# Query look-ups of an edge attention: one fp32 product a tile in place of three bf16 ones

## The chip, the core and the metric

One core of a Trainium2 chip runs one program. The core has TensorE (matrix products, written to PSUM), VectorE, ScalarE, GpSimd and SyncE, which run their own instruction streams and wait for each other by semaphores. The metric is the device time of one execution in microseconds; less is better.

## The reference

The program is a graph network of four parts over 3125 nodes with 128 features and 53125 edges (25000 random ones, their reverses, and a self-loop at each node), sorted by target `dst`: ten propagation steps, two graph attention layers, a relational layer, and a transformer layer on edges. Between the parts stands a layer norm of x plus the part's result. The change lies in the last two. The relational layer adds to x a weighted sum over edges and normalizes x. The attention then computes:

```
Q = (x @ Wq).reshape(n, 8, 16); K, V likewise
score = K[src] * Q[dst] / sqrt(16)
s = exp(clip(sum(score, -1), -5, 5))
wV = segment_sum(V[src] * s, dst); z = segment_sum(s, dst)
h = (wV / (z + 1e-6)) @ Wo + bo, then x + h, two batch norms and a two-layer MLP
```

## The kernel before

Nodes are cut into NB = 25 blocks of 128. The edges of a block fill CAP = 18 tiles of 128 edges, and 8 in the last block: 440 tiles. The blocks are also grouped into seven sets (five of 4 blocks, one of 2, one of 3); after a set the next part's matrix products for its nodes are slipped in between blocks.

**Relations** (L2246 to L2320). GpSimd gathers for each tile 128 rows from a table in HBM (L2265) into a ring `rows` of three blocks. VectorE makes one-hot matrices of the targets (L2299). TensorE adds up each tile by a product of the one-hot matrix with the rows (L2286), in fp32; after each six tiles (a group) a matmul increments `summed`, for which GpSimd waits before it reuses those slots of the ring. VectorE closes a block (L2307, L2309) and, at the end of a set, normalizes it. Then **IntoCross** makes keys, values and queries of that set: TensorE transposes x (L2185), ScalarE copies the transpose (L2205), TensorE multiplies each block by the three weight matrices together (L2193, 384 columns, two PSUM banks `pr` in turn), ScalarE copies the 384 columns into a ring `kvq` (L2215, semaphore `out`) and stores keys and values to a table in HBM (L2218). VectorE splits the queries into three bf16 parts whose sum is the fp32 value (L2232, L2235, L2238, L2241) into `own`, and increments `split`. In the last set keys and values come first and the queries after them (L2197, L2223).

**Cross** is the attention. Its engines run these loops over the blocks:

- GpSimd gathers keys and values of each tile (L2593) into the same ring `rows` of three blocks; each six tiles it waits for the sums that free the slots.
- SyncE sends the targets of a block, broadcast over the partitions, to `dst_wide`; ScalarE makes the transposed one-hot matrices `turned` of it by two passes (L1857, L1861), so that column e of `turned` picks the target's row for edge e.
- TensorE looks up the query of each edge: for each tile three bf16 matmuls with `turned` as the stationary operand and the three parts of the queries moving, added up in PSUM (L2623). Tiles are taken in groups of four (quads), five a block. The first three quads of block b + 1 are looked up before the sums of block b; the fourth and fifth come at the start of the next turn, since they reuse the banks of the first two. Each increments `looked`.
- VectorE multiplies the gathered keys by the looked-up queries (L2668), adds them up a head (L2673), clips (L2687), and, after ScalarE's exponentials (L2604, L2607), weighs the values (L2695), then makes the next one-hot matrices (L1824).
- TensorE adds up the weighed values (L2644, fp32, 136 columns). Every six tiles `summed` is incremented. VectorE closes the block (L2700 to L2702).

The order on TensorE in turn b is: quads 3 and 4 of block b, quads 0 to 2 of block b + 1, sums of block b. After each set of blocks some products of the next part come ahead of that.

```
            for j, tiles in enumerate(quads_of(b)):
                pe.wait_ge(self.ready, QUADS[b] + j + 1)
```

Of the kernel before, what the change touches and what calls it, by code (L numbers as in the profile page):

```python
# [1359 lines left out]
class Tiles:  # L1360


    def __init__(self, c, ctx, y):
# [45 lines left out]
        self.iota = self.top_ps[:, 384:384 + P]  # L1409
        self.weight = self.seen_ps[:, 432:432 + CAP * HEADS].rearrange("p (t h) -> p t h", h=HEADS)  # L1410

    def query(self, b):

        return self.own[:, b, :].bitcast(bf16)[:, 0:3 * D].rearrange("p (i f) -> p i f", i=3)
# [414 lines left out]
class TurnedHots:  # L1829
# [21 lines left out]
    def turn(self, act, b):  # L1851
# [9 lines left out]
        c.nc.scalar.activation(t.turned[:, b % 2, 0:n], t.apart[:, 0:n], ACT.Relu, bias=c.ones[:, 0:1], scale=-1.0).then_inc(self.turned_made, 1)  # L1861


class Layer(TurnedHots):
# [15 lines left out]
    def looked_after(self, b):  # L1880
        return b + 1

# [272 lines left out]
class IntoCross:  # L2155
# [3 lines left out]
    def __init__(self, c, t, table):  # L2159
        self.c, self.t, self.table = c, t, table  # L2160
        self.loaded, self.small, self.turned, self.copied, self.done, self.out, self.split, self.step = (
            c.sem(f"into_x_{n}") for n in ("loaded", "small", "turned", "copied", "products", "out", "split", "step"))
        self.tabled = [c.sem(f"into_x_tabled{h}") for h in range(2)]
        self.stored = [0, 0]
# [12 lines left out]
    def pe(self, pe, layer, i):  # L2177
# [11 lines left out]
        for j, b in enumerate(blocks):  # L2189
            if b >= 2:  # L2190
                pe.wait_ge(self.out, b - 1)
            n = 2 * D if at_end else 3 * D
            c.nc.tensor.matmul(t.pr[b % 2][:, 0:n], t.turned_all[:, j * P:(j + 1) * P], t.w_kvq[:, 0:n], start=True, stop=True).then_inc(self.done, 1)  # L2193
        if at_end:
            for j in range(len(blocks)):
                pe.wait_ge(self.out, NB + j - 1)
                c.nc.tensor.matmul(t.pr[(NB + j) % 2][:, 0:D], t.turned_all[:, j * P:(j + 1) * P], t.w_kvq[:, 2 * D:3 * D], start=True, stop=True).then_inc(self.done, 1)  # L2197

    def act(self, act, layer, i):
# [7 lines left out]
        n = 2 * D if at_end else 3 * D  # L2207
        for piece in pieces_of(blocks):
            half = piece[0] // 4 % 2
            for b in piece:  # L2210
                if b >= 8 and b % 4 == 0:
                    act.wait_ge(self.tabled[half], 16 * self.stored[half])
                    act.wait_ge(self.split, b // 4 - 1)
                act.wait_ge(self.done, b + 1)
                c.nc.scalar.copy(t.kvq[:, b % 8, 0:n], t.pr[b % 2][:, 0:n]).then_inc(self.out, 1)  # L2215
# [4 lines left out]
        if at_end:  # L2220
            for j, b in enumerate(blocks):
                act.wait_ge(self.done, NB + j + 1)
                c.nc.scalar.copy(t.kvq[:, b % 8, 2 * D:3 * D], t.pr[(NB + j) % 2][:, 0:D]).then_inc(self.out, 1)  # L2223

    def dve(self, dve, layer, i):
        c, t, blocks, v = self.c, self.t, SETS[i], self.c.nc.vector
        pieces = [(t.kvq[:, p[0] % 8:p[0] % 8 + len(p), 2 * D:], [t.own[:, p[0]:p[-1] + 1, :].bitcast(bf16)[:, :, n * D:(n + 1) * D] for n in range(3)])
                  for p in pieces_of(blocks)]
        dve.wait_ge(self.out, blocks[-1] + 1 + (len(blocks) if i == len(SETS) - 1 else 0))
        then = chained(dve, self.step, 3 * i)  # L2230
        for query, parts in pieces:
            last = v.tensor_copy(parts[0], query)  # L2232
        then(last)
        for query, parts in pieces:
            last = v.tensor_tensor(query, query, parts[0], ALU.subtract)  # L2235
        then(last)
        for query, parts in pieces:
            last = v.tensor_copy(parts[1], query)  # L2238
        then(last)
        for query, parts in pieces:  # L2240
            last = v.tensor_tensor(parts[2], query, parts[1], ALU.subtract)  # L2241
        last.then_inc(self.split, 1)


class Relations:
# [45 lines left out]
    def dve(self, dve, own_out):  # L2291
# [22 lines left out]
        for b in range(NB):  # L2314
            if b + 1 < NB:
                make_hots(b + 1)
            if b - 1 in SET_DONE:
                self.after.dve(dve, self, SET_DONE[b - 1])
            close(b)
        self.after.dve(dve, self, len(SETS) - 1)  # L2320
# [243 lines left out]
class Cross(TurnedHots):  # L2564
# [3 lines left out]
    def __init__(self, c, t, table, tabled, split, after):  # L2568
        self.c, self.t, self.table, self.tabled, self.split, self.after = c, t, table, tabled, split, after
# [6 lines left out]
    def looked_after(self, b):  # L2576
        return LOOKED[b + 1]

# [35 lines left out]
    def pe(self, pe):  # L2614
        c, t = self.c, self.t

        def look_up(b, lo, hi):
            pe.wait_ge(self.turned_made, b + 1)
            query = t.query(b)
            for j in range(lo, min(hi, len(quads_of(b)))):  # L2620
                for m, n in enumerate(quads_of(b)[j]):
                    for i in range(3):
# [985 lines left out]
```

## Time and profile before

| | |
|---|---|
| runs | 4167.31, 4172.69, 4187.54 us, median 4172.69 |
| profiled execution, span from first to last instruction | 4173.0 us (no other time is given for it) |
| TensorE, VectorE, GpSimd busy | 61%, 51%, 42% of the span |
| relation stage, first to last gather | 2781.0 to 3397.2 us |
| attention stage, first to last gather | 3423.3 to 4084.2 us |
| mean granted TensorE clock | 0.765 of full speed |

In the rows below PE is TensorE's matmuls and PEld its weight loads, DVE VectorE, ACT ScalarE, POOL GpSimd. The start of a matmul in the trace is when it entered TensorE's stream; its end is modelled. In brackets stands the idle time of the engine before an instruction and what ended it: "issue" means that it waited for nothing that the profile shows, "remote" that the releaser was not found.

### The profile page before, as it was taken

To read this page: it belongs to the slowest core of one execution; us is meant where nothing else is said; L and a number is where in the kernel's file an instruction comes from. 1 tells how busy PE (TensorE), PEld (TensorE's weight loads), DVE (VectorE), ACT (ScalarE), POOL (GpSimd) and SP (SyncE) were. 2 spreads that over 40 slices of the span, in tenths; PEclk is the share of its full clock that TensorE was granted. 3 is DMA by queue.
4 is the path that set the end of the run, shared out by engine and by line. 5 is a ranking of instruction groups with operands and counts; after the bars stand their busy time and mean duration, and the time that the engine had idled before them with its cause. 6 is when DMAs were issued, how large, how long until landed. Compare 5 with 4: busy or idle time off the path is not lost.

```text
span 4173.0 us, 49514 instructions
## 1 busy us (share of the span) xinstructions
PE 2540.6 (61%) x14597; PEld 1791.1 (43%) x14598; DVE 2114.5 (51%) x5736; ACT 725.1 (17%) x1115; POOL 1742.4 (42%) x1837
## 2 busy tenths in 40 slices
PE   5879999999996355565245555552333343444446
PEld 3546666666664244344134333432222232444445
DVE  8975555555554365566255455651222233444446
ACT  5840000000002132222122222210000011112112
POOL 2210000000002666664565555526666656666660
PEclk9989999999998677676567776775555665666667
DMA  2000000000004444442344343321111123333331
GB/s 63 1 1 0 0 0 0 0 0 0 0 0 123 112 118 125 116 123 78 109 116 125 113 117 112 112 60 47 50 52 52 52 70 104 105 109 107 109 112 28
DMA packets 139378, 283.86 MB, mean 68 GB/s; under 512 B 35752, under 2 KB 79124, under 8 KB 139156
## 3 DMA queue, kind: packets, MB, share of 16 engines
q0 software_dynamic: 77760, 204.68, 17.8%
q1 hardware_dynamic: 24603, 53.25, 4.0%
q10 hardware_dynamic: 36864, 24.07, 1.9%
q8 instruction: 76, 1.25, 0.1%
q14 instruction: 75, 0.61, 0.0%
HBM read 255.10 MB, written 27.01 MB: 68 GB/s over the span
## 4 chain that ended last, share of the span: by engine, by line
issue 20%; PE 14%; DVE 14%; another core or an unknown queue 11%; POOL 6%; ACT 2%; DMA 1%; SPq 0%; DVEq 0%; ACTq 0%; POOLq 0%
PE t_sum_ps L1996 7%; POOL t_rows L2265 6%; DVE t_onehot L1824 2%; PE t_product_ps L1665 2%; DVE t_rows L2078 2%; DVE t_stage L2668 1%; DVE t_stage L2673 1%; DVE t_rows L2695 1%; PE t_sum_ps L2286 1%; ACT t_apart L1857 1%; PE t_small_ps L1966 1%; PE t_product_ps L1590 0%; POOL t_rows L2593 0%; DVE t_norm_pair L1335 0%
## 5 line engine op out<-in xcount | busy, mean ns | idle before, releaser
L1896 POOL DMA_INDIRECT t_rows<-gat_table,t_src x880 | 837.9, 952 | 572.0 <-issue 254.0
L1038 PE MATMUL hop_ps<-parts,counts 128*128 128x384 bf16 (+1 forms) x6150 | 1003.3, 326 | 2.2 <-DVE parts L1099 2.2
L1038 PEld LDWEIGHTS hop_ps<-parts,counts 128*128 (+1 forms) x6150 | 603.4, 98 | 402.2 <-issue 10.2
L1996 PE MATMUL t_sum_ps<-t_rows,t_onehot 128*128 128x264 f32 x1760 | 540.6, 465 | 258.4 <-issue 210.3
L1996 PEld LDWEIGHTS t_sum_ps<-t_rows,t_onehot 128*128 128x128 f32 x1760 | 405.0, 234 | 367.9 <-issue 286.9
L2265 POOL DMA_INDIRECT t_rows<-rel_table_b,t_rel x440 | 418.9, 952 | 272.7 <-issue 129.8
L2593 POOL DMA_INDIRECT t_rows<-kv_table_b,t_src x440 | 416.0, 945 | 271.0 <-issue 127.0
L1465 POOL IOTA t_node<- 128x1 f32 x1 | 0.1, 131 | 1040.5 <-POOLq L106 1040.5
L2286 PE MATMUL t_sum_ps<-t_rows,t_onehot 128*128 128x128 f32 x880 | 174.6, 340 | 334.6 <-issue 283.9
L2286 PEld LDWEIGHTS t_sum_ps<-t_rows,t_onehot 128*128 128x128 f32 x880 | 155.7, 251 | 356.7 <-issue 356.2
L2644 PE MATMUL t_sum_ps<-t_rows,t_onehot 128*128 128x136 f32 x880 | 185.8, 366 | 152.9 <-issue 152.1
L2078 DVE TENSOR_TENSOR t_rows<-t_rows,t_sum_ps 128x768 f32<-128x768 f32 x288 | 253.2, 947 | 17.6 <-issue 9.8
L2668 DVE TENSOR_TENSOR t_stage<-t_rows,t_small_ps 128x512 f32<-128x512 f32 x98 | 58.6, 619 | 368.0 <-remote 332.5
L2644 PEld LDWEIGHTS t_sum_ps<-t_rows,t_onehot 128*128 128x128 f32 x880 | 169.2, 270 | 173.9 <-issue 173.4
L1107 DVE TENSOR_REDUCE s_new<-hop_ps 128x128 f32<-128x384 f32 (+1 forms) x225 | 125.5, 558 | 220.9 <-PE hop_ps L1038 212.2
L2623 PE MATMUL t_small_ps<-t_own,t_turned 128*128 128x128 bf16 x1032 | 90.3, 262 | 206.1 <-issue 180.3
L2307 DVE TENSOR_TENSOR t_own<-t_own,t_sum_ps 128x128 f32<-128x128 f32 x25 | 7.2, 287 | 407.8 <-remote 383.1
L1824 DVE TENSOR_TENSOR t_onehot<-t_small_ps,t_dst 128x768 f32<-128x768 f32 x222 | 196.9, 941 | 1.8 <-DVE y_fast L2099 0.6
L929 PE MATMUL cnt_ps<-hot_column,hot_src 128*128 128x320 bf16 x880 | 160.5, 320 | 39.1 <-DVE hot_column L973 34.9
L1474 ACT COPY t_turned_all<-t_turn_ps 128x512 f32<-128x512 f32 (+1 forms) x4 | 2.2, 558 | 1022.9 <-PE t_turn_ps L1508 1021.4
L2623 PEld LDWEIGHTS t_small_ps<-t_own,t_turned 128*128 128x128 bf16 x1032 | 81.5, 120 | 214.3 <-issue 192.2
L1857 ACT ACTIVATE t_apart<-t_dst_wide,t_node 128x2304 f16<-128x2304 f16 (+1 forms) x75 | 161.9, 2158 | 19.9 <-DMA t_dst_wide<-dst_row 19.6
(366 smaller groups left out, 3013.1 us busy)
## 6 DMA issues: line engine op xcount, KB each, us to landing
t_dst_wide<-dst_row SPq DMA_DIRECT2D x72, 576.0 KB
t_rows<-gat_table,t_src POOLq DMA_INDIRECT x880
rel_table_b<-t_stage ACTq DMA_DIRECT2D x25, 512.0 KB, 3.2
t_rows<-rel_table_b,t_rel POOLq DMA_INDIRECT x440
t_rows<-kv_table_b,t_src POOLq DMA_INDIRECT x440
gat_table<-t_own ACTq DMA_DIRECT2D x10, 520.0 KB, 6.5
kv_table_b<-t_fresh ACTq DMA_DIRECT2D x5, 512.0 KB
out<-x SPq DMA_DIRECT2D x6, 256.0 KB
```

What stands on the lines that cost most here:

```text
L929: last = nc.tensor.matmul(bank[:, h * 512:h * 512 + JH], hot_src[:, g % 2, :, n], hot[:, k % RING, h * JH:(h + 1) * JH], start=(k == ks[0] ...
L1038: last = nc.tensor.matmul(ps[bank][0:m, 0:PARTS * D], counts[:, k, columns], parts[old][:, k, :], start=(k == 0), stop=(k == NB - 1))
L1824: last = v.tensor_tensor(t.onehot[:, hot_at(ks[lo]):hot_at(ks[lo]) + m, :], t.iota.rearrange("p (o d) -> p o d", o=1).to_broadcast([P, m, P]),
L1857: c.nc.scalar.activation(t.apart[:, 0:n], t.dst_wide[:, b % 2, 0:n], ACT.Abs, bias=t.node[:, 0:1], scale=-1.0).then_inc(self.apart_made, 1)
L1896: c.nc.gpsimd.indirect_dma_start(t.rows[:, slot(k), 0:FW], None, self.table, bass.IndirectOffsetOnAxis(ap=t.src[:, k:k + 1], axis=0)).then ...
L1996: product = c.nc.tensor.matmul(t.pa[b % 2][:, 0:RW], t.onehot[:, hot_at(k), :], t.rows[:, slot(k), :], start=(n == 0), stop=(n == len(ks) ...
L2078: v.tensor_tensor(h, h, self.weight(b)[:, tiles[0]:tiles[0] + m, :].rearrange("p t (h o) -> p t h o", o=1).to_broadcast([P, m, HEADS, HID] ...
L2265: c.nc.gpsimd.indirect_dma_start(t.rows[:, slot(k), 0:D], None, self.table, bass.IndirectOffsetOnAxis(ap=t.rel[:, k:k + 1], axis=0)).then_ ...
L2286: product = c.nc.tensor.matmul(t.pa[b % 2][:, 0:D], t.onehot[:, hot_at(k), :], t.rows[:, slot(k), 0:D], start=(n == 0), stop=(n == len(ks) ...
L2593: c.nc.gpsimd.indirect_dma_start(t.rows[:, slot(k), 0:2 * D], None, self.table, bass.IndirectOffsetOnAxis(ap=t.src[:, k:k + 1], axis=0)).t ...
L2623: last = c.nc.tensor.matmul(self.looked_ps[j][:, m * P:(m + 1) * P], t.turned[:, b % 2, n * P:(n + 1) * P], query[:, i, :], start=(i == 0) ...
L2644: product = c.nc.tensor.matmul(t.pa[b % 2][:, 0:D + XH], t.onehot[:, hot_at(k), :], t.rows[:, slot(k), D:2 * D + XH], start=(n == 0), stop ...
```

## The change

A query is kept as one fp32 row and no longer split. ScalarE copies the query columns out of PSUM by an instruction of its own, straight into `queries`, a packed array in the memory of `own` (semaphore `asked`); the copy into the ring `kvq` shrinks to 256 columns. VectorE's four splitting operations a set and the semaphore `split` go. TensorE waits for `asked` as well as `out` before it reuses a bank `pr`. In the attention the transposed one-hot matrices are fp32: one buffer takes the memory of both bf16 ones, the other a free part of `own`. The look-up is one fp32 matmul a tile in place of three bf16 ones.

```diff
@@ -1407,11 +1407,10 @@
         self.pt = c.banks(ctx, "t_turn_ps", 1)[0]
         self.pr = c.banks(ctx, "t_product_ps", 2)
         self.iota = self.top_ps[:, 384:384 + P]
+        nodes = self.own[:, :, :].rearrange("p b f -> p (b f)")
+        self.queries = nodes[:, 0:NB * D].rearrange("p (b f) -> p b f", f=D)
+        self.turned_wide = [self.turned[:, :, :].rearrange("p q e -> p (q e)").bitcast(f32), nodes[:, NB * D:NB * D + CAP * P]]
         self.weight = self.seen_ps[:, 432:432 + CAP * HEADS].rearrange("p (t h) -> p t h", h=HEADS)
-
-    def query(self, b):
-
-        return self.own[:, b, :].bitcast(bf16)[:, 0:3 * D].rearrange("p (i f) -> p i f", i=3)
 
 
 def parts_of_scores(c, then, t, blocks):
@@ -1858,7 +1857,7 @@
         act.wait_ge(self.apart_made, b + 1)
         if b >= 2:
             act.wait_ge(self.looked, self.looked_after(b - 2))
-        c.nc.scalar.activation(t.turned[:, b % 2, 0:n], t.apart[:, 0:n], ACT.Relu, bias=c.ones[:, 0:1], scale=-1.0).then_inc(self.turned_made, 1)
+        c.nc.scalar.activation(self.turned_at(b)[:, 0:n], t.apart[:, 0:n], ACT.Relu, bias=c.ones[:, 0:1], scale=-1.0).then_inc(self.turned_made, 1)
 
 
 class Layer(TurnedHots):
@@ -1879,6 +1878,9 @@
 
     def looked_after(self, b):
         return b + 1
+
+    def turned_at(self, b):
+        return self.t.turned[:, b % 2, :]
 
     def weight(self, b):
 
@@ -2158,8 +2160,8 @@
 
     def __init__(self, c, t, table):
         self.c, self.t, self.table = c, t, table
-        self.loaded, self.small, self.turned, self.copied, self.done, self.out, self.split, self.step = (
-            c.sem(f"into_x_{n}") for n in ("loaded", "small", "turned", "copied", "products", "out", "split", "step"))
+        self.loaded, self.small, self.turned, self.copied, self.done, self.out, self.asked = (
+            c.sem(f"into_x_{n}") for n in ("loaded", "small", "turned", "copied", "products", "out", "asked"))
         self.tabled = [c.sem(f"into_x_tabled{h}") for h in range(2)]
         self.stored = [0, 0]
 
@@ -2189,11 +2191,14 @@
         for j, b in enumerate(blocks):
             if b >= 2:
                 pe.wait_ge(self.out, b - 1)
+                pe.wait_ge(self.asked, min(b - 1, blocks[0] if at_end else b - 1))
             n = 2 * D if at_end else 3 * D
             c.nc.tensor.matmul(t.pr[b % 2][:, 0:n], t.turned_all[:, j * P:(j + 1) * P], t.w_kvq[:, 0:n], start=True, stop=True).then_inc(self.done, 1)
         if at_end:
             for j in range(len(blocks)):
-                pe.wait_ge(self.out, NB + j - 1)
+                pe.wait_ge(self.out, min(NB + j - 1, NB))
+                if j >= 2:
+                    pe.wait_ge(self.asked, blocks[0] + j - 1)
                 c.nc.tensor.matmul(t.pr[(NB + j) % 2][:, 0:D], t.turned_all[:, j * P:(j + 1) * P], t.w_kvq[:, 2 * D:3 * D], start=True, stop=True).then_inc(self.done, 1)
 
     def act(self, act, layer, i):
@@ -2204,15 +2209,15 @@
             act.wait_ge(self.done, blocks[0])
         c.nc.scalar.copy(t.turned_all[:, 0:m], t.pt[:, 0:m]).then_inc(self.copied, 1)
         at_end = i == len(SETS) - 1
-        n = 2 * D if at_end else 3 * D
         for piece in pieces_of(blocks):
             half = piece[0] // 4 % 2
             for b in piece:
                 if b >= 8 and b % 4 == 0:
                     act.wait_ge(self.tabled[half], 16 * self.stored[half])
-                    act.wait_ge(self.split, b // 4 - 1)
                 act.wait_ge(self.done, b + 1)
-                c.nc.scalar.copy(t.kvq[:, b % 8, 0:n], t.pr[b % 2][:, 0:n]).then_inc(self.out, 1)
+                c.nc.scalar.copy(t.kvq[:, b % 8, 0:2 * D], t.pr[b % 2][:, 0:2 * D]).then_inc(self.out, 1)
+                if not at_end:
+                    c.nc.scalar.copy(t.queries[:, b, :], t.pr[b % 2][:, 2 * D:3 * D]).then_inc(self.asked, 1)
             act.wait_ge(self.out, piece[-1] + 1)
             lo, m = piece[0], len(piece)
             act.dma_start(self.table[lo * P:(lo + m) * P, :].rearrange("(b p) f -> p b f", p=P), t.kvq[:, lo % 8:lo % 8 + m, 0:2 * D]).then_inc(self.tabled[half], 16)
@@ -2220,26 +2225,7 @@
         if at_end:
             for j, b in enumerate(blocks):
                 act.wait_ge(self.done, NB + j + 1)
-                c.nc.scalar.copy(t.kvq[:, b % 8, 2 * D:3 * D], t.pr[(NB + j) % 2][:, 0:D]).then_inc(self.out, 1)
-
-    def dve(self, dve, layer, i):
-        c, t, blocks, v = self.c, self.t, SETS[i], self.c.nc.vector
-        pieces = [(t.kvq[:, p[0] % 8:p[0] % 8 + len(p), 2 * D:], [t.own[:, p[0]:p[-1] + 1, :].bitcast(bf16)[:, :, n * D:(n + 1) * D] for n in range(3)])
-                  for p in pieces_of(blocks)]
-        dve.wait_ge(self.out, blocks[-1] + 1 + (len(blocks) if i == len(SETS) - 1 else 0))
-        then = chained(dve, self.step, 3 * i)
-        for query, parts in pieces:
-            last = v.tensor_copy(parts[0], query)
-        then(last)
-        for query, parts in pieces:
-            last = v.tensor_tensor(query, query, parts[0], ALU.subtract)
-        then(last)
-        for query, parts in pieces:
-            last = v.tensor_copy(parts[1], query)
-        then(last)
-        for query, parts in pieces:
-            last = v.tensor_tensor(parts[2], query, parts[1], ALU.subtract)
-        last.then_inc(self.split, 1)
+                c.nc.scalar.copy(t.queries[:, b, :], t.pr[(NB + j) % 2][:, 0:D]).then_inc(self.asked, 1)
 
 
 class Relations:
@@ -2314,10 +2300,7 @@
         for b in range(NB):
             if b + 1 < NB:
                 make_hots(b + 1)
-            if b - 1 in SET_DONE:
-                self.after.dve(dve, self, SET_DONE[b - 1])
             close(b)
-        self.after.dve(dve, self, len(SETS) - 1)
 
 
 class IntoSum:
@@ -2565,8 +2548,8 @@
 
 
 
-    def __init__(self, c, t, table, tabled, split, after):
-        self.c, self.t, self.table, self.tabled, self.split, self.after = c, t, table, tabled, split, after
+    def __init__(self, c, t, table, tabled, asked, after):
+        self.c, self.t, self.table, self.tabled, self.asked, self.after = c, t, table, tabled, asked, after
         super().__init__(c, "cross")
         self.step, self.hot, self.viewed, self.reduced, self.clipped, self.exped, self.ready, self.summed, self.freed = (
             c.sem(f"cross_{n}") for n in ("step", "hot", "viewed", "reduced", "clipped", "exped", "ready", "summed", "freed"))
@@ -2575,6 +2558,9 @@
 
     def looked_after(self, b):
         return LOOKED[b + 1]
+
+    def turned_at(self, b):
+        return self.t.turned_wide[b % 2]
 
     def weight(self, b):
 
@@ -2616,13 +2602,11 @@
 
         def look_up(b, lo, hi):
             pe.wait_ge(self.turned_made, b + 1)
-            query = t.query(b)
             for j in range(lo, min(hi, len(quads_of(b)))):
                 for m, n in enumerate(quads_of(b)[j]):
-                    for i in range(3):
-                        last = c.nc.tensor.matmul(self.looked_ps[j][:, m * P:(m + 1) * P], t.turned[:, b % 2, n * P:(n + 1) * P], query[:, i, :], start=(i == 0), stop=(i == 2))
+                    last = c.nc.tensor.matmul(self.looked_ps[j][:, m * P:(m + 1) * P], self.turned_at(b)[:, n * P:(n + 1) * P], t.queries[:, b, :], start=True, stop=True)
             last.then_inc(self.looked, 1)
-        pe.wait_ge(self.split, len(SETS))
+        pe.wait_ge(self.asked, NB)
         look_up(0, 0, AHEAD)
         for b in range(NB):
             for i in AFTER_CROSS.get(b, []):
@@ -2742,7 +2726,7 @@
         into_sum = IntoSum(c, t, into_cross.small)
         last = Finish(c, t, into_sum, [(leave.x_done, 3 * NB)])
         relations = Relations(c, t, rel_table, leave.tabled, into_cross)
-        cross = Cross(c, t, kv_table, into_cross.tabled, into_cross.split, into_sum)
+        cross = Cross(c, t, kv_table, into_cross.tabled, into_cross.asked, into_sum)
         with every_engine(nc) as block:
             @block.sync
             def _(sp):
```

## Rows read from the trace of the kernel before

**Rows 1.** The page, its first line.

```profile
span 4173.0 us, 49514 instructions
```

**Rows 2.** Busy time of each engine in the attention stage.

```profile
core 0: us, PE busy (x) PEld busy (x) DVE busy (x) ACT busy (x) POOL busy (x), PEclk, DMA share, GB/s
3423.00:4085.00 662.00, 294.33 (x2132) 268.87 (x2133) 279.27 (x514) 124.56 (x104) 415.78 (x440) 0.65 0.36 108
```

**Rows 3.** The wait list of the attention stage: total us, times, longest.

```profile
DVE t_stage L2668 <- remote: 332.5, 55, 15.5
...
POOL t_rows L2593 <- PE t_sum_ps L2644: 119.0, 22, 11.0
```

**Rows 4.** Timeline of one block of the attention: start us, us, engine, line.

```profile
3782.82 1.88 PE L2623 MATMUL t_small_ps<-t_own,t_turned 128*128 128x128 bf16 x24 [3.72 <-issue]
...
3787.28 0.26 PE L2623 MATMUL t_product_ps<-t_own,t_turned 128*128 128x128 bf16 x1 [1.16 <-issue]
...
3795.11 0.95 POOL L2593 DMA_INDIRECT t_rows<-kv_table_b,t_src  x1 [0.30 <-issue]
...
3797.77 7.51 PE L2644 MATMUL t_sum_ps<-t_rows,t_onehot 128*128 128x136 f32 x31 [0.32 <-issue]
...
3799.16 5.91 PEld L2644 LDWEIGHTS t_sum_ps<-t_rows,t_onehot 128*128 128x128 f32 x29 [0.41 <-issue]
3799.55 1.28 DVE L2668 TENSOR_TENSOR t_stage<-t_rows,t_small_ps 128x512 f32<-128x512 f32 x2 [9.13 <-remote]
...
3800.94 0.94 POOL L2593 DMA_INDIRECT t_rows<-kv_table_b,t_src  x1 [4.88 <-PE t_sum_ps L2644]
```

**Rows 5.** Timeline of a block that follows a set's products.

```profile
3834.45 1.17 PE L2623 MATMUL t_small_ps<-t_own,t_turned 128*128 128x128 bf16 x18
...
3841.97 0.69 DVE L2668 TENSOR_TENSOR t_stage<-t_rows,t_small_ps 128x512 f32<-128x512 f32 x1 [12.04 <-remote]
...
3850.37 0.42 DVE L2668 TENSOR_TENSOR t_stage<-t_rows,t_small_ps 128x256 f32<-128x256 f32 x1 [7.12 <-remote]
...
3850.85 2.74 PE L2623 MATMUL t_small_ps<-t_own,t_turned 128*128 128x128 bf16 x24 [15.23 <-issue]
...
3856.95 0.94 POOL L2593 DMA_INDIRECT t_rows<-kv_table_b,t_src  x1 [6.94 <-PE t_sum_ps L2644]
```

**Rows 6.** Timeline of the first block of the attention.

```profile
3464.66 0.69 DVE L2668 TENSOR_TENSOR t_stage<-t_rows,t_small_ps 128x512 f32<-128x512 f32 x1 [14.13 <-remote]
...
3481.46 0.42 DVE L2668 TENSOR_TENSOR t_stage<-t_rows,t_small_ps 128x256 f32<-128x256 f32 x1 [15.52 <-remote]
...
3499.25 1.28 DVE L2668 TENSOR_TENSOR t_stage<-t_rows,t_small_ps 128x512 f32<-128x512 f32 x2 [10.20 <-issue]
...
3501.42 0.94 POOL L2593 DMA_INDIRECT t_rows<-kv_table_b,t_src  x1 [10.97 <-PE t_sum_ps L2644]
```

**Rows 7.** The wait list of the graph layers, GpSimd.

```profile
POOL t_rows L1896 <- remote: 102.1, 29, 7.9
```

**Rows 8.** Groups by form, attention stage: count, busy us, mean ns.

```profile
L2644 PE MATMUL t_sum_ps<-t_rows,t_onehot 128*128 128x136 f32 x880 | 185.8, 366 | 152.9 <-issue 152.1
...
L1861 ACT ACTIVATE t_turned<-t_apart,ones 128x2304 bf16<-128x2304 f16 x24 | 53.2, 2215 | 0.8
```

**Rows 9.** Timeline of sums in the relation stage.

```profile
3095.02 0.37 PE L2286 MATMUL t_sum_ps<-t_rows,t_onehot 128*128 128x128 f32 x1 [2.43 <-issue]
...
3119.52 4.64 PE L2286 MATMUL t_sum_ps<-t_rows,t_onehot 128*128 128x128 f32 x21 [0.33 <-issue]
...
3119.69 0.29 DVE L2307 TENSOR_TENSOR t_own<-t_own,t_sum_ps 128x128 f32<-128x128 f32 x1 [38.83 <-remote]
```

**Rows 10.** Groups by form, relation stage: copies out of PSUM, splitting.

```profile
L2215 ACT COPY t_fresh<-t_product_ps 128x384 f32<-128x384 f32 x22 | 10.5, 478 | 23.8 <-PE t_product_ps L2193 13.0 <-issue 7.4 <-remote 3.4
...
L2232 DVE CAST t_own<-t_fresh 128x512 bf16<-128x512 f32 x5 | 2.4, 472 | 12.7 <-issue 11.3 <-ACT t_fresh L2215 1.4
...
L2223 ACT COPY t_fresh<-t_product_ps 128x128 f32<-128x128 f32 x3 | 0.8, 265 | 0.7 <-ACT t_fresh L2215 0.4 <-PE t_product_ps L2197 0.2
```

## Prediction

> **What bounds the kernel now.** I read the page first, then the stages, the wait list, the groups by form, and last the timeline of single blocks. The profiled execution spans 4173.0 us [rows 1]. The change touches two stages. In the attention stage (3423 to 4085 us) TensorE is busy 294 of 662 us, VectorE 279, ScalarE 125 and GpSimd 416 [rows 2]. No engine is full there, so the waits decide. GpSimd issues one gather a tile: 0.95 us and a gap of 0.30 [rows 4], 1.25 us apiece, so the 440 need 550 of the 662 us and a block of 18 tiles 22.5. The rest is in the wait list: GpSimd stood 119.0 us in 22 waits for TensorE's sums, which free the ring of gathered rows; VectorE stood 332.5 us in 55 waits put down to "remote" [rows 3]. The loop is: gather, look-up, sum, ring free, gather.
>
> The timeline of one block shows what these waits are. From 3782.82 the 36 look-up matmuls of three groups are recorded (24, 11 and 1). After some 70 records (35 matmuls and their weight loads) the stream breaks into single steps of 0.7 or 1.4 us. The last look-up matmul is recorded at 3787.28, yet VectorE, which waits only for it, starts at 3799.55, 12 us later. GpSimd's last gather ran 3795.11 to 3796.06, and TensorE's stream runs freely again from about 3799. GpSimd goes on at 3800.94, after the first six tiles' sums [rows 4]. The 18 look-ups recorded from 3834.45, all in the stream by 3835.6, release VectorE at 3841.97 (12 matmuls) and 3850.37 (6 more): the last six, 12 records, took 8.4 us with nothing else on TensorE, 0.70 us a record [rows 5]. In the first block the same six took 16.8 us, from 3464.66 to 3481.46, 1.4 us a record [rows 6]. I read this so: while gathers flow, TensorE may run some 70 instructions ahead, but their completions come out at 0.7 to 1.4 us each. When the gathers stop for lack of ring slots, everything held back comes out at once. The Trainium skill (TensorE: Matmul & The Clock Gate, the table at its head) gives TensorE's engine queue a depth of 64; the trace's 70 agree with it roughly.
>
> The graph layers before it, with the same ring, show the floor of this loop: 29 waits of GpSimd took 102.1 us, 3.5 us each [rows 7]. That is the wait when the ring-freeing signal comes out together with the clearing. In the attention stage a wait is 4.88 us in a regular block and 6.94 in one that follows a set's products, every fourth [rows 4, 5]; the 22 average 5.4 [rows 3]. They are longer than 3.5 because some sums of the first group still have to run after the clearing.
>
> **The change, part by part.** *Look-ups.* They go from three bf16 matmuls a tile (1320 of them) to one fp32 matmul. An fp32 product is two weight loads and two matmuls in the records: L2644 has 880 matmuls for 440 tiles [rows 8]. Records per tile go from 6 to 4, for 18 tiles from 108 to 72, for the 12 tiles looked up ahead from 72 to 48.
>
> Array time goes the other way. At half clock (1.2 GHz) 24 bf16 matmuls took 2.74 us, less some 0.3 us for the last one's own length, over 23, 0.106 us each, 0.32 us a tile [rows 5]; 21 fp32 ones of 128 columns took 4.64 us, so 0.211 us each, 0.42 us a tile [rows 9]. So 440 tiles cost 44 to 47 us more of array, 22 at full clock. The Trainium skill (FP8 and Floating Point Precision, TensorE Precision Notes) says the same against this change: true FP32 takes 4 passes, against the three of bf16 parts. The trace agrees, 0.42 to 0.32. By that rule alone the stage gets slower by up to 47 us, by the count of records it gets faster.
>
> Which one is on the path? Block at 3782.8: 72 look-up records must come before the first group of sums (24 records). Of the 36 weight loads of the sums 29 are recorded from 3799.16 on, and of the 36 matmuls 31 from 3797.77 on [rows 4]. So at the clearing 72 + some 15 records had entered, 87 in all, and the rest of group 0 ran after it: wait 4.88. With 48 look-up records, 87 covers all 24 records of the group (72) with room. Their array time, 12 x 0.42 + 6 x 0.46 = 7.8 us, fits the 16 us between 3782.8 and the clearing. So the signal comes with the clearing, wait 3.5 us, as in the layers. Gain 1.4 in a block like this one. Of 119.0 us the first wait (10.97 [rows 6]) and five long ones of 6.9 leave 73.5 for the 16 regular ones, 4.6 each, so 1.1 on average, 18 us in all.
>
> The long one (6.94): the 12 look-ups behind the late start took 7.5 us, the six after 8.4. By records these become 5.0 and 5.6, so VectorE gets the last at 3845.1 in place of 3850.37. The 12 tiles of the next block start at 3845.6 and take 5.1 us, 3850.7; the six tiles of sums take 2.7 more, 3853.4. The last gather ended at 3850.0 and the clearing comes 3.3 us after, 3853.3. GpSimd resumes near 3853.8: wait about 4.0, gain 2.9, five times: 14 us. The first wait (clearing at 3499.25, resumption at 3501.42 [rows 6]) gains about 2. Sum: 18 + 14 + 2 = 34 us. From above it is bounded by all waits at 3.5: 119.0 - 21 x 3.5 - 9.0 = 36.5 us (the first wait ends at the clearing, 3499.4). From below, if fp32 records complete half as fast as bf16 ones, nothing is gained and the 33% more of array comes on top: a loss, taken below as a rival.
>
> Which row speaks of the speed of fp32 completions? In the relation stage, all fp32, a matmul stepped in 2.8 us after the one before (2.43 idle + 0.37), 1.4 us a record, and VectorE's sum came at 3119.69 after 38.83 us [rows 9]. That is bf16's worst (1.4), not twice it. I take them as equal per record.
>
> *Tail.* After the last gather nothing is held back, and the array time is on the path: the last block's 24 look-ups, at most the 2.74 us of [rows 5], become about 3.4 (8 x 0.42), and the 18 ones before them 6 x 0.1 more: +1.2 us.
>
> *ScalarE.* `turned` is written in fp32 in place of bf16. Its pass over 2304 elements takes 2.215 us with bf16 out [rows 8], 0.96 ns an element; I take the same for fp32, since the copies with fp32 out run at the like (0.48 us for 384, 0.27 for 128: 0.83 ns an element and a fixed part [rows 10]). 25 blocks of them lie in ScalarE's idle time (125 of 662 us busy [rows 2]). The transfers of `dst_wide` on SyncE's queue are not touched. If that cover were wrong and fp32 doubled it, 2.2 us a block would still fit.
>
> *Relations.* The copy of 384 columns (0.48 us, x22) becomes one of 256 (between 0.27 and 0.48) and one of 128 (0.27): +0.06 to +0.27 us of work, in the 22 blocks outside the last set [rows 10]. TensorE now waits for the second copy. Each product is two matmuls of 384 columns, by 0.211 us for 128 at half clock 1.27 us [rows 9], and there are two banks, so the two copies (0.75 us at most) hide behind the next product; uncovered they would cost 22 x 0.27 = 6 us. I take +1. The splitting goes from VectorE, four operations a set, the first 0.47 us for 512 columns [rows 10], some 2 us a set and 15 in all. VectorE waits for sums there, 38.83 us at one go [rows 9]; after the last set the first look-up needs `turned` from ScalarE too, two passes of 2.2 us, which cover the split. The wait for the split before reuse of the store ring goes as well. Gain 0 to 2; I take 0.
>
> Total: -34 + 1.2 + 1 = -31.8. I take 30 off, for a few waits that stay long, since each step uses completion rates that the rows give only as 0.7 to 1.4: **4143 us**. The span, 4173.0, equals the median of the runs (4172.69), so the sum stands against either.
>
> **Rivals.**
> *Completion follows the passes (slower).* If what is slowed is the array's passes, four for three, then the work of 12 tiles after the clearing grows by 12 x 0.106 = 1.3 us a block (28 us over 22 waits, at full clock half of it), and in the long blocks the 15.9 us of look-ups grow by a third, 5.3 us, some four times: 20 more. 4173 + 14, up to + 48: 4187 to 4221. For it: a pair of fp32 records took 2.8 us in the relation stage where six bf16 pairs took 1.4 each [rows 5, 9]. Against: the first block's bf16 pairs also took 2.8 [rows 6]. It decides as soon as an fp32 record completes over 1.5 times slower than a bf16 one.
> *The two cancel.* Fewer records, but each somewhat slower: the waits stay at 4 to 5 us. 4160 to 4185, the likeliest value 4170.
> *It does less than it says, but helps.* The clearing happens later as more sums are held back; only the regular waits shorten: 10 to 15 us, 4158 to 4163. I count it to the second.
>
> **Chances.** A change of 0.5% (21 us) is about what a measurement tells from none. Faster by the first case 0.57; within it 0.22 (second and third); slower 0.21 (first rival). Its own range is 4132 to 4152. Over all, leaving out the upper half of the slow rival and a little below, 4130 to 4203.
>
> **What the profile after would show.** Right: look-ups as 880 weight loads and 880 matmuls of fp32, GpSimd's waits for sums down from 119 to about 85 us, the regular ones at 3.5, the attention stage near 630 us from first to last gather in place of 661, the relation stage at 617 unchanged within 3. Wrong: waits of GpSimd at 6 or more in every block, VectorE's late look-ups (7.12 us now) above 10, or a relation stage that grew, which would put TensorE's wait for the second copy on the path.

## The result

The kernel after takes 4135.9 us (median of 4 runs, 4125.4 to 4139.0), the kernel before 4173.4 (4 runs, 4167.3 to 4187.5): a ratio of 0.9919, with a 95% interval of 0.9893 to 0.9945. The forecast was 4143. The profiled execution of after took 4135.2 us, with a span of 4133.5.

In each fence below the view of after stands that answers to rows of before. First the page's span and the windows view of the attention stage (as [rows 1, 2]):

```profile
span 4133.5 us, 48641 instructions
...
3422.00:4048.00 626.00, 333.70 (x1723) 287.83 (x1724) 277.17 (x507) 126.73 (x106) 417.14 (x440) 0.68 0.38 114
```

TensorE is busy 334 us, 39 more than before, in a stage that is 36 us shorter: first to last gather 625.3 us (3422.2 to 4047.5) against 660.9. The wait list of after tells where they came from (total us, times, longest; as [rows 3]):

```profile
DVE t_stage L2652 <- remote: 159.4, 20, 11.7
DVE t_stage L2652 <- PE t_small_ps L2607: 74.3, 14, 9.8
DVE t_stage L2652 <- issue: 69.6, 6, 35.2
POOL t_rows L2579 <- remote: 63.8, 17, 8.3
POOL t_rows L2579 <- PE t_sum_ps L2628: 17.8, 5, 3.6
```

L2579 is the gather, L2607 the look-up, L2628 the sums, L2652 the multiplication. GpSimd's 22 waits for sums are now put down to two releasers; together they are 81.6 us, before 119.0. The groups by form of after show the look-ups and the one-hot pass (as [rows 8]):

```profile
L2607 PE MATMUL t_small_ps<-t_own,t_turned 128*128 128x128 f32 x336 | 60.2, 350 | 36.9 <-DVE t_stage L2652 23.4 <-issue 8.5 <-ACT t_turned L1860 4.8
L1860 ACT ACTIVATE t_turned<-t_apart,ones 128x2304 f32<-128x2304 f16 x12 | 26.6, 2218 | 0.4
```

The timeline of after, the end of the first block's wait (as [rows 6]), and the block behind a set's products (as [rows 5]):

```profile
3497.93 0.95 POOL L2579 DMA_INDIRECT t_rows<-kv_table_b,t_src  x1 [8.35 <-remote]
...
3707.05 1.50 PE L2607 MATMUL t_small_ps<-t_own 128*128 128x128 f32 x12
3708.14 0.69 DVE L2652 TENSOR_TENSOR t_stage<-t_rows,t_small_ps 128x512 f32<-128x512 f32 x1 [9.69 <-PE t_small_ps L2607]
3709.53 0.42 DVE L2652 TENSOR_TENSOR t_stage<-t_rows,t_small_ps 128x256 f32<-128x256 f32 x1
3710.00 2.05 PE L2607 MATMUL t_small_ps<-t_own,t_turned 128*128 128x128 f32 x16 [1.46 <-issue]
...
3729.12 2.65 PE L2628 MATMUL t_sum_ps<-t_rows,t_onehot 128*128 128x136 f32 x11 [0.31 <-issue]
...
3729.55 0.95 POOL L2579 DMA_INDIRECT t_rows<-kv_table_b,t_src  x1 [3.58 <-remote]
```

VectorE gets its late look-ups 1.1 us after they enter TensorE and the last two tiles right behind, 1.39 us later, which is its own work. Before, those two tiles came 8.40 us after the four ahead of them [rows 5]. GpSimd waits 3.58 us there; in the block of [rows 5] it was 6.94.

### The profile page after: what moved, and what is told of

Its sections match the earlier page's. It is cut to its first block, busy times and chain, and to the rows that moved or that the text cites. A ratio compares the mean times of both kernels' runs of the same rounds, so it can differ in the third digit from the quotient of the medians.

```text
span 4133.5 us, 48641 instructions
## 1 busy us (share of the span) xinstructions
PE 2570.8 (62%) x14157; PEld 1797.3 (43%) x14158; DVE 2101.2 (51%) x5704; ACT 727.7 (18%) x1137; POOL 1747.5 (42%) x1837
## 4 chain that ended last, share of the span: by engine, by line
issue 27%; PE 17%; DVE 10%; another core or an unknown queue 6%; POOL 4%; ACT 3%; DMA 0%; ACTq 0%; DVEq 0%
PE t_sum_ps L1998 7%; POOL t_rows L2251 4%; PE t_sum_ps L2628 2%; DVE t_rows L2080 2%; PE t_small_ps L2607 1%; PE t_product_ps L1664 1%; PE t_sum_ps L2272 1%; DVE t_onehot L1823 1%; ACT t_apart L1856 1%; DVE t_stage L2652 1%; DVE t_stage L2657 1%; DVE t_rows L2679 1%; PE t_small_ps L1968 1%; PE t_product_ps L2196 0%
## 5 line engine op out<-in xcount | busy, mean ns | idle before, releaser
L1998 PE MATMUL t_sum_ps<-t_rows,t_onehot 128*128 128x264 f32 x1760 | 550.3, 472 | 253.1 <-issue 202.2
L1998 PEld LDWEIGHTS t_sum_ps<-t_rows,t_onehot 128*128 128x128 f32 x1760 | 409.9, 237 | 367.3 <-issue 284.5
L2579 POOL DMA_INDIRECT t_rows<-kv_table_b,t_src x440 | 417.6, 949 | 232.5 <-issue 127.1
L2628 PE MATMUL t_sum_ps<-t_rows,t_onehot 128*128 128x136 f32 x880 | 185.6, 330 | 237.5 <-issue 232.8
L2272 PEld LDWEIGHTS t_sum_ps<-t_rows,t_onehot 128*128 128x128 f32 x880 | 147.3, 241 | 331.4 <-issue 329.8
L2628 PEld LDWEIGHTS t_sum_ps<-t_rows,t_onehot 128*128 128x128 f32 x880 | 147.0, 223 | 271.9 <-issue 270.8
L2652 DVE TENSOR_TENSOR t_stage<-t_rows,t_small_ps 128x512 f32<-128x512 f32 x98 | 58.7, 621 | 338.0 <-remote 159.4
L973 DVE TENSOR_SCALAR hot_column<-iota_c,cnt_column,cnt_unit 128x640 bf16<-128x640 f16 x367 | 156.8, 491 | 2.5 <-PE cnt_ps L929 2.2
L1664 PE MATMUL t_product_ps<-t_w_rel,t_turned_all 128*128 128x512 f32 x132 | 73.6, 696 | 111.6 <-ACT t_turned_all L1740 61.8
```

Of the source, the lines that this page charges most:

```text
L973: v.tensor_scalar(hot[:, k % RING, :], iota_c[:, :], column[:, k:k + 1], unit[:, k:k + 1], ALU.is_equal, ALU.mult).then_inc(dve_hot, 1)
L1998: product = c.nc.tensor.matmul(t.pa[b % 2][:, 0:RW], t.onehot[:, hot_at(k), :], t.rows[:, slot(k), :], start=(n == 0), stop=(n == len(ks) ...
L2272: product = c.nc.tensor.matmul(t.pa[b % 2][:, 0:D], t.onehot[:, hot_at(k), :], t.rows[:, slot(k), 0:D], start=(n == 0), stop=(n == len(ks) ...
L2579: c.nc.gpsimd.indirect_dma_start(t.rows[:, slot(k), 0:2 * D], None, self.table, bass.IndirectOffsetOnAxis(ap=t.src[:, k:k + 1], axis=0)).t ...
L2628: product = c.nc.tensor.matmul(t.pa[b % 2][:, 0:D + XH], t.onehot[:, hot_at(k), :], t.rows[:, slot(k), D:2 * D + XH], start=(n == 0), stop ...
```

## The experiments

The theory to test: while gathers flow, TensorE's completions come at a price per instruction record (weight load or matmul), whatever its format and array time. Rivals: array passes count; the gain comes from making the queries in another way; it comes from a higher granted clock (0.771 over the span, before 0.765).

**Four variants of the look-up.** The edits, the first two on the kernel before, the others on the kernel after (`...` marks cuts, and operands are given by short names):

```diff
 # two_parts_b                                  (one_part_b: range(1), stop=(i == 0))
-                    for i in range(3):
+                    for i in range(2):
-  ... start=(i == 0), stop=(i == 2))
+  ... start=(i == 0), stop=(i == 1))
 # tiny_b, ahead of each fp32 look-up; half and query are the upper halves of the fp32 words
+                    c.nc.tensor.matmul(into[:, 0:8], half, query[:, 0:8], start=True, stop=True)
 # into_only_b: three bf16 look-ups on t.turned in place of the fp32 one
+                    for i in range(3):
+                        last = c.nc.tensor.matmul(into, turned, query, start=(i == 0), stop=(i == 2))
```

> The kernel before with two bf16 look-up matmuls a tile in place of three (the third part of the queries is left out of the product, everything else of IntoCross stays as it was). 4 records a tile as after, 2 passes of the array in place of 4. By records (my theory): the same gain as the change, GpSimd's waits for sums near 3.5 us each, 82 to 90 in all, 4136 within 10 us. By array passes (rival): less work than after, so faster than after by 10 us or more, below 4126. If the gain came from how the queries are made and not from the look-ups (rival): no gain, near 4173.

> The kernel before with a single bf16 look-up matmul a tile (two parts of the queries left out). 2 records a tile, 1 pass. By records, with a floor: a wait of GpSimd is 3.5 us at least, because it ends with the clearing, so only the first wait and the tail can still shorten: 4125 to 4137, waits 77 to 82 in all. If there is no floor and what counts is the amount of work on TensorE: twice the gain of two parts, near 4100.

> The kernel after with one more matmul a tile, bf16, 8 columns, into the columns that the true look-up overwrites: 6 records a tile as before, with almost no work for the array. By records: the gain is lost, waits of GpSimd 4.9 us and more in regular blocks and about 7 in those behind a set's products, 4165 to 4180. By array passes: no change against after, 4136 within 5.

> The kernel after with before's look-ups: bf16 turned one-hot matrices and three bf16 matmuls a tile, each reading the upper halves of the fp32 queries (so the product is of queries cut to bf16, three times). It has the change's way to make and keep the queries and none of its saving of records. By records: the attention stage as before, 661 us, regular waits 4.9; the relation stage shows what the second ScalarE copy costs, 617 to 622: 4173 to 4178 in all. If the gain came from the dropped splitting: near 4140.

None of this could be read, because the chip behaved otherwise: the kernel before itself took 3696.9 us there (31 runs), and the ratios were 0.9997, 0.9995, 0.9991 and 0.9995, each within 0.0010. Between one bf16 pass a tile and four and more fp32 passes lies nothing that can be measured. The line view of the gathers of two_parts_b, and its windows view of the attention stage, show why:

```profile
L2593 POOL DMA_INDIRECT t_rows<-kv_table_b,t_src x440: 940/946/1392, 3067.6 to 3618.5; - x147
its engine sat idle before it (us, times) until:
  issue: 131.6, 432
...
  PE t_sum_ps L2644: 2.1, 7
```
```profile
3067.00:3620.00 553.00, 234.67 (x1790) 214.52 (x1791) 295.76 (x543) 128.73 (x111) 418.11 (x440) 0.66 0.43 129
```

440 gathers in 550.9 us are 1.25 us apiece, the issue of GpSimd and nothing else; its waits for sums are 2.1 us in all. The kernel into_only_b runs the look-ups of before on this chip, in records as in passes. Its timeline in the first block:

```profile
3093.31 1.29 DVE L2653 TENSOR_TENSOR t_stage<-t_rows,t_small_ps 128x512 f32<-128x512 f32 x2 [28.28 <-DMA t_rows<-kv_table_b,t_src]
3094.05 2.10 PE L2608 MATMUL t_small_ps<-t_own,t_turned 128*128 128x128 bf16 x18 [16.69 <-DVE t_stage L2653]
...
3096.68 0.69 DVE L2653 TENSOR_TENSOR t_stage<-t_rows,t_small_ps 128x512 f32<-128x512 f32 x1
...
3098.07 0.42 DVE L2653 TENSOR_TENSOR t_stage<-t_rows,t_small_ps 128x256 f32<-128x256 f32 x1
```

The last two tiles' queries are there 1.39 us after the four before, at a full stream of gathers. On the chip of the profile before, the same six bf16 matmuls took 16.80 us in the same place (3464.66 to 3481.46, [rows 6]). Holding back completions is thus no property of the program or of gathers as such: on this chip it doesn't happen.

**The change again, and the look-up done twice.** The second kernel changes the look-up of after (short names again):

```diff
-  last = matmul(into, wide, query, start=True, stop=True)
+  matmul(into, wide, query, start=True, stop=False)
+  last = matmul(into, wide, query, start=False, stop=True)
```

> The kernel after, unchanged, beside the kernel before on the same chip. The four runs before this one showed a chip on which the kernel before takes 3697 us, GpSimd never waits for a sum and nothing is held back. My theory now: the gain exists only where completions are held back while gathers flow. If the kernel before takes 3697 us again: a ratio within 0.1% of 1. If it takes 4173 us: a ratio near 0.992, GpSimd's waits for sums 78 to 86 us. Rival: the gain of 0.8% was a matter of chance between executions, and the ratio is 1 on any chip.

> The kernel after with every look-up done twice and added up (8 records and 8 passes a tile; the scores are doubled). If the kernel before takes 3697 us on this chip: gathers alone set the pace, the extra 47 us of array hide, no wait of GpSimd, within 0.2% of before, but for some 3 us in the tail. If it takes 4173 us: by records 96 look-up records go ahead of the sums in place of 72 before, waits longer than before, 4190 to 4230; by array passes rather than records about the same or more, so this one tells size and not cause.

These two ran on a chip that does hold back: before took 4166.2 us (8 runs). The change again: 4136.2 us, ratio 0.9927 (0.9900 to 0.9954), waits of GpSimd for sums 61.6 + 21.4 = 83.0 us. The gain is repeated where completions are held back. Twice: 4220.8 us, ratio 1.0142 (1.0113 to 1.0172), GpSimd's waits:

```profile
L2579 POOL DMA_INDIRECT t_rows<-kv_table_b,t_src x440: 943/949/1095, 3421.9 to 4126.5; - x147
its engine sat idle before it (us, times) until:
  PE t_sum_ps L2629: 161.1, 22
```

The time is in the range given, and the waits (7.1 us apiece without the first) are longer than before, as said. Its granted clock, 0.782, was the highest of the four profiled executions on such chips (before 0.765, after 0.771 and 0.769), and its time the longest: a higher clock doesn't by itself make this kernel shorter. And its first block bears on records against passes after all, by VectorE's starts on the last four and the last two tiles:

```profile
3468.60 0.69 DVE L2653 TENSOR_TENSOR t_stage<-t_rows,t_small_ps 128x512 f32<-128x512 f32 x1 [19.40 <-issue]
3491.00 0.42 DVE L2653 TENSOR_TENSOR t_stage<-t_rows,t_small_ps 128x256 f32<-128x256 f32 x1 [21.12 <-remote]
```

The last two tiles are 16 records here (eight fp32 matmuls and their weight loads) and took 22.40 us: 1.40 us a record. Before they were 12 records of bf16, in 16.80 us [rows 6]: 1.40 us a record. By passes, 16 against 6, it would have been 44.8 us. TensorE's own starts show the same step, here in the first block of before (bf16 look-ups) and of after (fp32 sums):

```profile
3488.45 0.10 PEld L2623 LDWEIGHTS t_product_ps<-t_own,t_turned 128*128 128x128 bf16 x1 [3.08 <-issue]
...
3489.86 0.27 PE L2623 MATMUL t_product_ps<-t_own,t_turned 128*128 128x128 bf16 x1 [2.55 <-issue]
```
```profile
3479.31 0.29 PEld L2628 LDWEIGHTS t_sum_ps<-t_rows,t_onehot 128*128 128x128 f32 x1 [2.51 <-issue]
...
3480.71 0.39 PE L2628 MATMUL t_sum_ps<-t_rows,t_onehot 128*128 128x136 f32 x1 [2.42 <-issue]
```

A record has one price here, bf16 or fp32, weight load or matmul. It isn't 1.40 us everywhere: the last two tiles in the first block of after, 8 records, came 5.29 us behind the four before them (3449.55 and 3454.84), since part of their records passed freely.

**The two kernels that tell records from passes, twice more.** The same files as two_parts_b and tiny_b:

> The kernel before with two bf16 look-up matmuls a tile in place of three (the third part of the queries is left out of the product, everything of IntoCross stays as it was), once more, for a chip on which the kernel before takes 4170 us. 4 records a tile as after, 2 passes of the array in place of 4. By records (my theory): the gain of the change, GpSimd's waits for sums near 3.5 us each and 80 to 90 in all, ratio 0.990 to 0.994. By array passes (rival): less work than after, ratio below 0.989. If the gain came from how the queries are made (rival): ratio 1. On a chip where before takes 3697 us: ratio 1 in every case.

> The kernel after with one more matmul a tile, bf16, 8 columns, into columns that the true look-up overwrites: 6 records a tile as before, 4 passes and a little of the array. Once more, for a chip on which the kernel before takes 4170 us. By records: the gain is lost, regular waits of GpSimd 4.9 us and more, ratio 0.998 to 1.006. By array passes: no change against after, ratio near 0.993. On a chip where before takes 3697 us: ratio 1 in every case.

> The kernel after with one more matmul a tile, bf16, 8 columns, into columns that the true look-up overwrites: 6 records a tile as before, 4 passes and a little of the array. For a chip on which the kernel before takes 4170 us, as the one of the repeat did. By records (my theory): the gain is lost, GpSimd's waits for sums 110 us or more in all, regular ones 4.9, ratio 0.998 to 1.006. By array passes: no change against after, waits near 83 us, ratio near 0.993. On a chip where before takes 3697 us: ratio 1 by either.

> The kernel before with two bf16 look-up matmuls a tile in place of three (the third part of the queries is left out of the product, everything of IntoCross stays as it was). 4 records a tile as after, 2 passes of the array in place of 4. For a chip on which the kernel before takes 4170 us. By records: the gain of the change without its IntoCross part, GpSimd's waits 80 to 90 us in all, ratio 0.990 to 0.994. By array passes: less work than after, ratio below 0.989. If the gain came from how the queries are made: ratio 1. On a chip where before takes 3697 us: ratio 1 by each.

Both pairs fell on chips where before takes 3701.6 and 3695.3 us. Ratios: 0.9995, 0.9995, 0.9995 and 1.0000, each within 0.0010. They are firm for such chips and don't tell records and passes apart.

**Four kinds of look-up in one execution.** The edit on after, `kind` being (matmuls of 8 columns, bf16 matmuls) by block:

```diff
+KINDS = {b: kind for first, kind in ((6, (1, 0)), (10, (0, 3)), (14, (0, 2)), (18, (2, 0))) for b in range(first, first + 4)}
+  for i in range(kind[0]): matmul(into[:, 0:8], half, query[:, 0:8], start=True, stop=True)
+  for i in range(kind[1]): last = matmul(into, half, query, start=(i == 0), stop=(i == kind[1] - 1))
+  if kind[1] == 0: last = matmul(into, wide, t.queries[:, b, :], start=True, stop=True)
```

> The kernel after with other look-ups in four stretches of four blocks, so that one execution compares them. Blocks 6 to 9: one bf16 matmul of 8 columns more a tile, overwritten by the true one (6 records, 4 passes and a little). 10 to 13: three bf16 matmuls on the upper halves of turned and queries (6 records, 3 passes; queries cut to bf16). 14 to 17: two of them (4 records, 2 passes). 18 to 21: two matmuls of 8 columns beside the fp32 one (8 records, 4 passes and a little). All others as after. On a chip where before takes 4170 us the wait of GpSimd in a block shows it; those between two blocks of one kind count (three a stretch, waits 6 to 8, 10 to 12, 14 to 16 and 18 to 20, counted from 0). By records: 3.8 to 5.2 us in the first and second stretch as before, 3.5 in the third as after, 6.4 to 7.5 in the fourth as with the look-up done twice; some 12 to 20 us longer than after. By array passes: 3.5 in the first, the third and the fourth, as after. On a chip where before takes 3697 us: no waits, the same time as before.

> The kernel of the run before this one, once more, for a chip on which the kernel before takes 4170 us: the kernel after with other look-ups in four stretches of four blocks. Blocks 6 to 9: one bf16 matmul of 8 columns more a tile (6 records, 4 passes and a little). 10 to 13: three bf16 matmuls on the upper halves of turned and queries (6 records, 3 passes; queries cut to bf16). 14 to 17: two of them (4 records, 2 passes). 18 to 21: two matmuls of 8 columns beside the fp32 one (8 records, 4 passes and a little). GpSimd's waits 6 to 8, 10 to 12, 14 to 16 and 18 to 20, counted from 0, tell the kinds apart. By records: 3.8 to 5.2 us in the first and second stretch, 3.5 in the third, 6.4 to 7.5 in the fourth; 12 to 20 us longer than after. By array passes: 3.5 in the first, the third and the fourth. On a chip where before takes 3697 us: no waits, the same time as before.

Again two chips that hold nothing back (before 3692.9 and 3698.4 us): ratios 1.0000 (0.9989 to 1.0011) and 0.9996 (0.9985 to 1.0008), GpSimd's waits for sums 0.6 us in all. So no run shows what these kernels, or two_parts and tiny, do on a chip that holds back.

The experiments thus fell on six chips: on one the kernel before takes 4166 us and the change gains 0.7%; on five it takes 3693 to 3702 us. There neither tiny_b, which has the whole change and an extra matmul, nor the bf16 variants differ from before. The kernel after itself was never run there.

## Why the prediction was right, and where not

**What bounds the kernel.** Right for the chip of the profile: the loop through GpSimd's waits for sums. The new times of the waits account for the gain. Without the first (10.97) and the five long ones (6.79 on average) before had 16 waits of 4.63 us; after has 21 waits of 3.49 besides the first of 8.35. That is 16 x 1.14 = 18.3, 5 x 3.30 = 16.5 and 2.6, in all 37.4 us; the stage got 35.6 shorter, since gathers and gaps between them took 1.8 more. The forecast was 18 + 14 + 2 = 34.

**Records, not passes.** The traces of the chips that hold back show it. Count the records from the start of the look-ups ahead to the clearing, when all that was held back comes out (taken as 3.1 us after the end of GpSimd's last gather), in the 16 blocks that don't follow a set's products. In before, with bf16 look-ups, 83 to 95 had entered in 14.9 to 18.4 us. With the look-up twice, in fp32, it was 82 to 97 in 15.0 to 17.8 us. That is the same number of records, but some 50 passes of the array against some 90. The 87 of the forecast lie in both ranges. After they aren't a constant: its look-ups ahead start earlier, 19.1 to 21.7 us ahead of the clearing, and 110 to 120 records had entered, all of the first group's among them.

What is still due at the clearing makes the rest of the wait. In before 1 to 13 records up to the last of the first group were due, and a straight line through the 16 waits (3.83 to 5.15 us) is 3.75 us and 0.112 us a record, within 0.12 us each. With the look-up twice 23 to 38 were due; that line gives 7.05 us on average, and 6.99 was measured. In after none were due, and the waits lie at 3.14 to 3.65 us, the floor that the graph layers showed. What stays untested is a kernel in which only the number of records differs from before or after: those that would have shown it never ran on a chip that holds back.

The rival by passes forecast 4187 to 4221; it fell. The Trainium skill (FP8 and Floating Point Precision, TensorE Precision Notes) gives true FP32 four passes, and the trace agrees that the array has more to do: TensorE is busy 39 us more. Only, that work lies beside GpSimd's gathers. The making of the queries isn't the source of the gain either: it lies in the relation stage, and 35.6 of the 39.5 us by which the span fell lie in the attention stage.

**The long waits.** This term was mis-sized: 4.0 us forecast (its own times, 3853.8 less 3850.0, give 3.8), 3.58 measured (at 3729.55). The step that failed took the late look-ups as held back at 0.7 us a record (5.0 and 5.6 us). The rows of after show them free: 12 matmuls enter at 3707.05 and VectorE has them at 3708.14. The forecast scaled their own records, 24 for 36, and left out what goes ahead of them. Between GpSimd's resumption and the first late look-up 69 records entered in each of the five long blocks of before, in after 21 to 27, since nearly all sums of the last block had entered before the clearing. So in before the 36 stood behind some 70 records that had entered since gathers flowed again, in after the 24 behind fewer than 30. The 70 aren't a fixed limit: in the first block of before 72 stood ahead of the 36, entered 17 us earlier, and at 1.40 us apiece only the last 24 of the 36 fit between 3448.0 and 3481.46. Fewer records gain more than in proportion, because they also shorten what stands ahead of the next ones.

**The tail** had the wrong sign: forecast +1.2 us, measured from the last gather to the end 86.0 after and 86.6 in its repeat, against 88.8 before. The chain of the last block in after:

```profile
4055.37 1.60 PE L2607 MATMUL t_small_ps<-t_own 128*128 128x128 f32 x12 [2.01 <-DVE t_stage L2652]
...
4059.87 2.05 PE L2607 MATMUL t_small_ps<-t_own,t_turned 128*128 128x128 f32 x16 [2.89 <-DVE t_stage L2652]
```

The last look-ups start 12.4 us after the last gather (4047.5), before 14.8 us (4098.98 after 4084.2). What was held back at the last gather is less. On the chips without holding back no sign can be read: 72.6 to 73.9 us in the kernels with bf16 look-ups only, 71.5 and 72.9 in mixed_b and mixed, whose last blocks look up as after does, and 73.9 to 74.9 in the three with tiny, which have a matmul more.

**Relations and ScalarE.** Forecast +1 us and within 3. The profile of after seemed to refute it, 621.4 us in place of 616.2, and the forecast had named a relation stage that grew as a sign of being wrong. The repeat says no: 616.4, and 616.5 in the kernel with the look-up twice, which makes its queries in the same way. The 5.2 us were of one execution. The second ScalarE copy costs nothing that these show, as the cover named for it says. The fp32 one-hot pass took 2.218 us (2.215 before), as forecast.

**What the prediction didn't have** is that its main condition is one of the chip. On five of the six chips of the experiments, by the ratios of the kernels around it, its forecast of -30 us would have been wrong and "the same" right. Nothing in one profile could show that, and that the result came from a chip that holds back was not the forecast's doing.

## What to carry to other kernels

Where a wait is far longer than the work that it waits for, count the instructions in the queue ahead of the releasing one, and not only their array time: here two thirds of the records with a third more array time gained 0.8%. Before such a gain is believed, look at the kernel on more than one chip: it was there on one kind of chip, and on the other, where the loop ran at the gathers' issue rate, kernels with two to eight look-up records a tile had ratios of 0.9991 to 1.0000. And let a second profile of the same kernel judge a stage difference of some 5 us.

## What the runs showed of the hardware

Chips differ. The same program before took 4166 to 4173 us on some and 3693 to 3702 on others, 11% less. Up to the first gather of the graph layers they agree: it starts at 1320.0 us in the profile of before and at 1321.3 in two_parts_b. All of the difference comes once gathers flow: relations start at 2781.0 against 2500.9, and take 616.2 against 550.5; the attention stage takes 660.9 against 550.9. The transfers themselves aren't slow. The gathers' issue is 0.95 us and a gap of 0.30 on both, and VectorE's first multiplication, which waits for the first block's gathers, starts 24.0 us after the first of them on both (3423.3 and 3447.26 in before, 3069.3 and 3093.31 in into_only_b). What differs is TensorE: on the slower kind its instructions go on, past some 70 records in the block of [rows 4], in steps of 0.70 or 1.40 us as long as gathers flow, one price for bf16 and fp32, and VectorE sees results late: 32 us after the last of the late look-ups had entered in the first block of before (3449.8 to 3481.46), 40 us with the look-up twice (3451.3 to 3491.0). Why a chip does so no run here shows. Each of the six chips was measured at one time only, so the chip and the hour can't be told apart, and which chip gave the profiles of before and after isn't known.
